# Fused cross-attention and quantized FFN on one core: down products on full chunks, transposed spreading, gate weights scaled ahead of their turn, fewer warming products, a new order in every queue

## What is computed

```python
def _L0_xattn_ref(teacher_logits, teacher_features, Wq, bq, Wk, bk):
    query = einsum('bnc,dc->bnd', teacher_features, Wq) + bq
    key = einsum('bnc,dc->bnd', teacher_features, Wk) + bk
    attention = softmax(einsum('bnd,bmd->bnm', query, key), axis=-1)
    return einsum('bln,bmn->blm', teacher_logits, attention)

def _reorder_quantize_x(x, idx):
    scale = max(abs(x)) / GLOBAL_DIV
    xr = (x / scale)[:, idx]
    scale_x = max(abs(xr), axis=1, keepdims=True) / FP8_MAX
    return _fp8(xr / scale_x), scale_x, scale

def _qlinear(qx, scale_x, scale, W, idx, out_idx=None):
    Wr = W[:, idx]
    w_scale = max(abs(Wr), axis=1, keepdims=True) / FP8_MAX
    y = qx * scale_x @ (_fp8(Wr / w_scale) * w_scale).T * scale
    return y if out_idx is None else y[:, out_idx]

x = x + xattn(layernorm(x), ctx, Wq, bq, Wk, bk)          # x: 4 x 256 x 256, ctx: 4 x 256 x 128
h = layernorm(x)                                          # 1024 rows of 256
g, u = qlinear(h, w_gate), qlinear(h, w_up)               # 704 wide
x = x + qlinear(quantize(silu(g) * u), w_down)            # back to 256 wide
```

## Time and profile before

| | us |
|---|---|
| median of 3 runs | 79.1 (79.03 to 79.25) |
| the profiled execution's own time | 79.58 |
| its span, from the first to the last instruction | 77.8 |
| PE busy (share) | 69.9 (90%) |
| PEld, weight loads | 57.6 (74%) |
| DVE busy | 61.1 (79%) |
| ACT busy | 56.9 (73%) |
| POOL busy | 49.0 (63%) |

### The profile page before, as it was taken

How to read it: one execution, slowest core, us unless ns; L and a number is a source line. 1 busy time by engine, 2 the same in 40 slices (tenths; PEclk the granted TensorE clock), 3 DMA queues, 4 the chain that set the end, 5 groups by cost and what they waited for, 6 DMA issues and landing times.

```text
span 77.8 us, 1587 instructions
## 1 busy us (share of the span) xinstructions
PE 69.9 (90%) x520; PEld 57.6 (74%) x520; DVE 61.1 (79%) x159; ACT 56.9 (73%) x118; POOL 49.0 (63%) x78
## 2 busy tenths in 40 slices
PE   4999999799959999999999999996989979998940
PEld 4999548589938988999887997984765746676710
DVE  1059899899995999988599999808999999992060
ACT  6106899997899889896899997996288371695400
POOL 5103135369649055987989887899998975853330
PEclk9999999999999999999999999999999999999999
DMA  0999899910000000000000011210240101042204
GB/s 13 272 414 418 258 366 412 409 53 8 0 4 4 0 0 0 0 0 8 0 0 0 34 38 34 67 24 1 85 118 0 67 0 56 11 135 71 70 6 135
DMA packets 4088, 6.98 MB, mean 90 GB/s; under 512 B 656, under 2 KB 2448, under 8 KB 4080
## 3 DMA queue, kind: packets, MB, share of 16 engines
q1 hardware_dynamic: 3888, 6.53, 23.5%
q0 software_dynamic: 192, 0.36, 1.4%
HBM read 5.48 MB, written 1.41 MB: 89 GB/s over the span
## 4 chain that ended last, share of the span: by engine, by line
PE 47%; POOL 22%; ACT 12%; issue 9%; DVE 7%; POOLq 0%; DVEq 0%; ACTq 0%
PE gate_ps L1258 9%; POOL act_g L402 9%; POOL wd_scatter L335 8%; PE tT_ps L1086 7%; PE gate_ps L1162 3%; PE up_ps L1137 3%; PE bank_s L1241 3%; PE tT_ps L1209 3%; PE tT_ps L1073 3%; ACT act_g L591 2%; DVE grid_t L769 2%; PE bank_s L1185 2%; DVE y_sb L892 2%; POOL qxT_bf L395 2%; ACT kT L495 2%
## 5 line engine op out<-in xcount | busy, mean ns | idle before, releaser
L402 POOL TENSOR_TENSOR act_g<-act_g,up_scale 128x704 f32<-128x704 f32 x8 | 13.6, 1695 | 1.1 <-ACT act_g L591 1.0
L1162 PE MATMUL gate_ps<-w_hi,qxT 128*128 128x352 f32 x32 | 11.0, 345 | 0.3 <-ACT act_g L591 0.3
L1209 PE MATMUL tT_ps<-ident,sum_t 128*128 128x128 f32 x48 | 10.4, 283 | 0.3 <-ACT tT L613 0.2
L383 POOL TENSOR_TENSOR sum_w<-sum_w,grid_w 128x256 f32<-128x256 f32 x6 | 4.1, 683 | 10.2 <-DVE sum_w L772 10.2
L1162 PE MATMUL gate_ps<-w_lo,qxT 128*128 128x352 f32 x32 | 10.2, 322 | 0.0
L414 POOL TENSOR_TENSOR x_sb<-y_sb,x 128x256 f32<-128x256 f32 x7 | 6.6, 945 | 5.6 <-DVE y_sb L892 5.6
L857 DVE TENSOR_TENSOR t_sb<-up_ps,act_g 128x704 f32<-128x704 f32 x8 | 7.1, 885 | 3.6 <-POOL act_g L402 2.2
L1212 PE MATMUL tT_ps<-negidentb,grid_t 128*128 128x128 bf16 x48 | 9.6, 219 | 0.0
L613 ACT ACTIVATE tT<-tT_ps 128x768 bf16<-128x768 f32 x7 | 5.7, 808 | 4.9 <-PE tT_ps L1212 4.7
L1086 PE MATMUL tT_ps<-attT,xT 128*128 128x256 f32 x32 | 7.6, 381 | 0.9 <-issue 0.9
L548 ACT ACTIVATE grid_w<-wup_sb,s_w 128x256 bf16<-128x256 f32 x12 | 5.2, 497 | 4.3 <-DVE s_w L808 4.3
(11 more groups left out here) (117 smaller groups left out, 203.6 us busy)
## 6 DMA issues: line engine op xcount, KB each, us to landing
wup_sb<-w_gate_up_dram SPq DMA_DIRECT2D x3, 512.0 KB, 4.8
x_sb<-x_dram SPq DMA_DIRECT2D x4, 256.0 KB, 8.0
xT<-x_t_dram SPq DMA_DIRECT2D x2, 512.0 KB, 9.6
out_dram<-x_sb SPq DMA_DIRECT2D x8, 128.0 KB, 1.7
wdn_sb<-w_down_dram SPq DMA_DIRECT2D x1, 704.0 KB, 6.6
head_sb<-head_dram SPq DMA_DIRECT2D x1, 416.0 KB, 5.4
wdnT<-wd_scatter SPq DMA_DIRECT2D x6, 64.0 KB, 1.9
ctx_sb<-ctx_t_dram SPq DMA_DIRECT2D x1, 256.0 KB, 6.8
```

What stands on the lines that cost most here:

```text
L402: nc.gpsimd.tensor_tensor(act_g[:, i % NT], act_g[:, i % NT], up_scale[:, :], ALU.mult)\
L1162: last = nc.tensor.matmul(ps[:, h, 0:IH], qxT[:, b, c, j * P:(j + 1) * P].bitcast(F32R), w[:, c, a, h * IH:(h + 1) * IH].bitcast(F32R), st ...
L1209: nc.tensor.matmul(to, sum_t[:, i % NT, of], ident[:, :], start=True, stop=False, is_transpose=True)
```

## The change

The down products take all 128 partitions of every chunk. For the last chunk the 64 partitions that belong to chunk 4 are multiplied by zeros, which POOL writes once, and `load_down_back(5)` fills the other 64 partitions alone. The products that spread peaks carry the transpose flag. POOL multiplies the rounded gate weights by their peaks (`scale_up`, a TENSOR_SCALAR of 128x256 float32, six of them), so that `turn_up` is four transpositions and two products with the negative identity; the diagonal matrices (128x128, six of them) are gone. WARM_UP is 15 in place of 24. All the lists of calls are in a new order, that of the loads too.

```diff
--- before.py
+++ after.py
@@ -16,7 +16,7 @@
 LN_EPS = 1e-5
 GRID_SHIFT = 20
 LEAST = 1.5 * 2.0 ** -6
-WARM_UP = 24
+WARM_UP = 15
 SCALED_BY_ACT = (0, 3, 6, 7)
 SUMMED = (1, 2, 4, 5)
 
@@ -109,7 +109,6 @@
         grid_w = sb("grid_w", [P, KC, 2, N], BF16)
         sum_w = sb("sum_w", [P, KC, 2, N])
         q_w = sum_w
-        diag_w = sb("diag_w", [P, KC, 1, P])
         w_hi = sb("w_hi", [P, NC, 1, I])
         w_up = sb("w_up", [P, NC, I], BF16)
         qxT_bf = sb("qxT_bf", [P, B, NC, L], BF16)
@@ -233,7 +232,6 @@
         rowscale_done = sem("rowscale_done")
         yscale_done = sem("yscale_done")
         q_w_done = sem("q_w_done")
-        diag_w_done = sem("diag_w_done")
         out_ready = [sem(f"out_ready{i}") for i in range(T)]
 
         block = ctx.enter_context(nc.Block())
@@ -261,7 +259,7 @@
 
                 if k == 0:
                     sp.wait_ge(scattered, 16 * KC)
-                sp.dma_start(wdnT[:, k], wd_dram[chunk(k), :]).then_inc(wdnT_in, 16)
+                sp.dma_start(wdnT[P - fresh[k]:, k], wd_dram[P * k:P * k + fresh[k], :]).then_inc(wdnT_in, 16)
 
             def store(i):
                 sp.wait_ge(out_ready[i], 1)
@@ -274,17 +272,17 @@
                 sp.dma_start(idx_sb[:, :], down_idx).then_inc(idx_in, 16)
 
             load_up(0)
+            load_x(0)
+            load_head()
+            load_x(1)
+            load_ctx()
+            load_down()
+            load_up(2)
             load_up(1)
-            load_head()
-            load_down()
-            load_ctx()
-            load_x(1)
+            load_x(3)
+            load_idx()
             load_x(2)
-            load_x(0)
-            load_up(2)
-            load_idx()
             load_xT(0)
-            load_x(3)
             load_xT(1)
             load_down_back(0)
             load_down_back(1)
@@ -323,6 +321,7 @@
                                              base=0, pattern=[[-1, P]], channel_multiplier=1), "ident")
                 after("ident")
                 nc.gpsimd.tensor_copy(identb[:, :], ident[:, :])
+                nc.gpsimd.memset(wdnT[0:P - fresh[KC - 1], KC - 1], 0.0)
                 nc.gpsimd.tensor_scalar(negidentb[:, :], ident[:, :], -1.0, 1.0, ALU.mult, ALU.mult)\
                     .then_inc(consts_ready, 1)
 
@@ -380,14 +379,13 @@
 
             def subtract_up(k):
                 pool.wait_ge(sum_w_done, k + 1)
-                nc.gpsimd.tensor_tensor(q_w[:, k, 0], sum_w[:, k, 0], grid_w[:, k, 0], ALU.subtract).then_inc(q_w_done, 1)
-
-            def diag_up(k):
-                if k == 0:
-                    after("ident")
+                step(nc.gpsimd.tensor_tensor(q_w[:, k, 0], sum_w[:, k, 0], grid_w[:, k, 0], ALU.subtract), ("q_w", k))
+
+            def scale_up(k):
+                after(("q_w", k))
                 pool.wait_ge(peak_w_done, k // 2 + 1)
-                nc.gpsimd.tensor_scalar(diag_w[:, k, 0], ident[:, :], peak_w[:, k, 0:1], 1.0, ALU.mult, ALU.mult)\
-                    .then_inc(diag_w_done, 1)
+                nc.gpsimd.tensor_scalar(q_w[:, k, 0], q_w[:, k, 0], peak_w[:, k, 0:1], 1.0, ALU.mult, ALU.mult)\
+                    .then_inc(q_w_done, 1)
 
             def copy_qxT(b):
 
@@ -415,69 +413,69 @@
                     .then_inc(out_ready[i], 1)
 
             constants()
-            diag_up(0)
-            diag_up(1)
+            add_eps1(0)
+            subtract_up(1)
             subtract_up(0)
-            diag_up(2)
-            subtract_up(1)
-            diag_up(3)
-            subtract_up(2)
+            scale_up(0)
+            scale_up(1)
             normalise(0)
             normalise(1)
-            add_eps1(0)
             rstd1_of(0)
-            diag_up(4)
+            subtract_up(2)
             normalise(2)
+            add_eps1(1)
+            scale_up(2)
+            normalise(3)
+            add_eps2(0)
             subtract_up(3)
-            add_eps2(0)
-            normalise(3)
+            scale_up(3)
+            subtract_up(4)
+            scale_up(4)
             rstd2_of(0)
-            subtract_up(4)
-            diag_up(5)
+            rstd1_of(1)
             subtract_up(5)
-            add_eps1(1)
-            rowscale_of(0)
             add_eps2(1)
-            rstd1_of(1)
-            copy_qxT(0)
-            rstd2_of(1)
-            rowscale_of(1)
-            scale_act(0)
-            add_eps2(2)
-            copy_qxT(1)
-            scale_act(1)
-            rstd2_of(2)
-            scale_act(2)
+            scale_up(5)
             scatter(0)
             scatter(1)
+            add_eps2(2)
+            scatter(2)
+            rowscale_of(0)
+            rstd2_of(1)
+            scatter(3)
+            copy_qxT(0)
+            scale_act(0)
+            scatter(4)
+            rowscale_of(1)
+            scale_act(1)
+            copy_qxT(1)
+            scatter(5)
+            scale_act(2)
+            rstd2_of(2)
+            yscale_of(0)
+            yscale_of(1)
+            copy_qxT(2)
             rowscale_of(2)
-            scatter(2)
-            copy_qxT(2)
-            scatter(3)
-            scatter(4)
-            scatter(5)
             scale_act(3)
+            yscale_of(2)
+            scale_act(4)
             add_eps2(3)
-            scale_act(4)
+            yscale_of(3)
             rstd2_of(3)
             rowscale_of(3)
-            yscale_of(0)
             scale_act(5)
             copy_qxT(3)
+            yscale_of(4)
             scale_act(6)
             add_residual(0)
-            yscale_of(1)
-            yscale_of(2)
-            yscale_of(3)
+            add_residual(1)
+            yscale_of(5)
             scale_act(7)
-            yscale_of(4)
-            add_residual(1)
+            yscale_of(6)
             add_residual(2)
-            yscale_of(5)
-            yscale_of(6)
             add_residual(3)
+            add_residual(4)
             yscale_of(7)
-            add_residual(4)
             add_residual(5)
             add_residual(6)
...
@@ -1124,7 +1122,8 @@
             def turn_up(k):
 
                 pe.wait_ge(q_w_done, k + 1)
-                pe.wait_ge(diag_w_done, k + 1)
+                if k == 0:
+                    pe.wait_ge(consts_ready, 1)
                 if k >= 2:
                     pe.wait_ge(w_lo_done, k - 1)
                 elif k == 0:
@@ -1134,8 +1133,7 @@
                 for c in range(NC):
                     for a in range(2):
                         if a == 0:
-                            nc.tensor.matmul(wuT_ps[k % 2][:, c, a], q_w[:, k, a, c * P:(c + 1) * P],
-                                             diag_w[:, k, a], start=True, stop=True)
+                            nc.tensor.transpose(wuT_ps[k % 2][:, c, a], q_w[:, k, a, c * P:(c + 1) * P], ident[:, :])
                         else:
                             nc.tensor.matmul(wuT_ps[k % 2][:, c, a], sum_w[:, k, a, c * P:(c + 1) * P], ident[:, :],
                                              start=True, stop=False, is_transpose=True)
@@ -1150,7 +1148,7 @@
                 pe.wait_ge(peak_d_done, 1)
                 for a in range(2):
                     last = nc.tensor.matmul(spread_ps[:, a], peak_d[:, a:a + 1].to_broadcast([P, P]), ident[:, :],
-                                            start=True, stop=True)
+                                            start=True, stop=True, is_transpose=True)
                 last.then_inc(spread_ready, 1)
 
             def product(i, ps, a):
@@ -1183,7 +1181,8 @@
                     pe.wait_ge(exp_done, B)
                 for k in (range(0, HALF_CHUNKS) if h == 0 else range(HALF_CHUNKS, KC)):
                     last = nc.tensor.matmul(bank_s[:, 0, (k % HALF_CHUNKS) * P:(k % HALF_CHUNKS + 1) * P],
-                                            peak_w[:, k, 1:2].to_broadcast([P, P]), ident[:, :], start=True, stop=True)
+                                            peak_w[:, k, 1:2].to_broadcast([P, P]), ident[:, :], start=True, stop=True,
+                                            is_transpose=True)
                 last.then_inc(up_spread, 1)
 
             def up_product(i):
@@ -1238,7 +1237,7 @@
                     pe.wait_ge(y_scaled, i)
                 for k in range(KC):
 
-                    last = nc.tensor.matmul(y_ps[i], tT[P - fresh[k]:, i % 2, k], wdnT[P - fresh[k]:, k],
+                    last = nc.tensor.matmul(y_ps[i], tT[:, i % 2, k], wdnT[:, k],
                                             start=(k == 0), stop=(k == KC - 1))
                 last.then_inc(y_ready, 1)
 
@@ -1247,7 +1246,7 @@
                 if h == 0:
                     pe.wait_ge(qxT_evac, B)
                 for k in (range(0, HALF_CHUNKS) if h == 0 else range(HALF_CHUNKS, KC)):
-                    last = nc.tensor.matmul(y_ps[LAST], tT[P - fresh[k]:, LAST % 2, k], wdnT[P - fresh[k]:, k],
+                    last = nc.tensor.matmul(y_ps[LAST], tT[:, LAST % 2, k], wdnT[:, k],
```

(37 more changed lines are left out.)

191 lines of the change are left out of this document (94 added, 97 removed).

## The result

The changed kernel takes 81.44 us, median of 4 runs (81.06 to 82.2); the kernel before, on the same chip, 79.17 (79.03 to 79.27). The ratio is 1.03, 95% interval 1.0223 to 1.0376: 3% slower. A repeat with three other kernels beside it gave 1.0249 (1.0171 to 1.0326).

What follows compares the result with a forecast made beforehand. The prediction took a shared chain, with everything waiting for POOL in the middle. -0.55 us to the end of `sum_of_t(5)` and -0.4 in the tail sum to -0.95, median forecast 78.2 us; range 76.6 to 80.0.

Steps and rivals of the forecast that it cites:

- the tail: Behind `sum_of_t(5)`: only `down(6)` and the last down product follow the last turn, so 0.4 us less.
- `scale_act(6)` ends at 33.0 + 26.5 + 1.3 = 60.8: POOL's middle: start of `scatter(0)`, plus the sum of POOL's calls, plus hits by DVE sums; `hidden(6)` then at 60.9.
- PE's list has `down(0)` right behind `turn_x(3)`, so PE waits there: PE in the middle: waits for down weights landing at 54.0, reaching `turn_t(5)` at 65.0, 1.1 us below DVE's bound.
- I take 33.0: Start of POOL's first scatter, taken near the late end of 31.8 to 33.6 us.
- signs of being wrong: `scatter(0)` behind 34; DVE idle between 12 and 15; 421 ns PE record behind 6 us; `turn_t(5)` released by PE's queue.
- POOL late by every sum: The second rival: five DVE sum hits of 0.65 and the `rstd` calls delay POOL; +0.7 to +1.1, 80.0 us; chance 0.26.
- The start: Warming products end at 6.1 us, head lands at 6.4, projections start at 6.5, first exponential at about 12.7.
- The gain of 1.65 us: At the start: projections begin at 6.5 us in place of 8.14.
- The scatters ahead of `scale_act(0)` thus buy nothing by themselves: POOL's middle: `hidden(0)` goes from 37.8 to about 41.5 and later tiles catch up; only the down weights come forward.
- The 0.21 us gap: Wait ahead of the 64-row weight load in each down product; full partitions remove it, 8 x 0.21 = 1.7 us less.
- PE's 4 us: Less PE work from transpositions, spreading and full chunks, 4.0 us together; only what lies in the tail counts.
- The stretch from `hidden(6)` to the end of `sum_of_t(5)`: DVE near the end: 5.2 us against 5.8, keeping 0.5 of the grid's stall; ends at 66.1 against 66.65.

Runs made afterwards that it cites:

- c_best: The changed kernel with `grids_x(3)` ahead of `hidden(2)`, `yscale_of(3)` behind `scale_act(5)` and `ups(4)` ahead of `turn_x(3)`; ratio 0.9993 to the kernel before.
- a_grid3: The changed kernel with one DVE call moved, `grids_x(3)` behind `hidden(3)`; ratio 1.0078 to the kernel before.
- c_ups4: The changed kernel with `grids_x(3)` behind `peak_of_t(3)`, `yscale_of(3)` behind `scale_act(5)` and `ups(4)` ahead of `turn_x(3)` and `down(0)`; ratio 1.0027 to the kernel before.
- the two runs: c_best with diagonal matrices back in place of `scale_up`, ratio 0.9969 to the kernel before, and c_rstd, 1.0043.
- a_warm24: The changed kernel with 24 warming products in place of 15; ratio 1.0159 to the kernel before.
- a_oldload: The changed kernel with the loads in their old order and the calls that depend on them moved back; ratio 1.0389 to the kernel before.
- c_late: c_best with the six scatters moved back in POOL's list, two behind each of `scale_act(0)`, `scale_act(1)`, `scale_act(2)`; ratio 1.0283 to the kernel before.
- a_rows64: The changed kernel with the last chunk's down products on 64 partitions again; ratio 1.0255 to the kernel before.
- c_rstd: c_best with one POOL call moved, `rstd2_of(0)` behind `scatter(2)`; ratio 1.0043 to the kernel before.
- b_parts: The kernel before, in its own order, with full down chunks, spreading as transposition and `scale_up` in place of the diagonals; ratio 1.0066 to the kernel before.

## Why the prediction was wrong

**Sum of the error.** Up to the last `scale_y` the forecast was -0.95 us and the profile has +1.40: 2.35 us. `hidden(6)` accounts for 2.1 (63.02 against 60.9), the stretch behind it for -0.2, the tail for 0.4. The 2.1 are three terms: 1.12 for `scatter(0)` (34.12 against 33.0), 0.62 for POOL from there to the end of `scale_act(6)` (28.42 us against 26.5 + 1.3), and 0.38 for DVE's calls between that end and `hidden(6)`, for which the forecast had 0.1. The rest of the medians' difference stays open.

**The step that failed: "`scale_act(6)` ends at 33.0 + 26.5 + 1.3 = 60.8".** It ended at 62.54. The sum took POOL as a queue that never waits, and counted DVE's sums as the only calls that meet it. Not in it was the grid, of which the earlier trace rows had the same case at 1.04 us: `grids_x(3)` stands in DVE's new list between `peak_of_t(2)` and `hidden(3)`, and POOL's has two `scale_act` running there. It took 2.4 us more than in the kernel before, and POOL waited 1.68 us through `yscale_of(3)`. That the stretch came out only 0.62 over is because the rest of it was 1.06 less than summed (the eleven small calls of 0.2 are 2.2, not 2.4, and c_best, without the wait, took 26.95 in all); one error hid part of the other. a_grid3 gives 0.95 back by that one call. Next to it, the step "PE's list has `down(0)` right behind `turn_x(3)`, so PE waits there" named the right place and the wrong wait: the weights were in time, `turn_x(3)` itself was late, and with it `ups(4)`. c_ups4 and c_best give 0.56 more. Together 1.5 us of the 2.35.

**The other step: "I take 33.0" for `scatter(0)`.** It came at 34.12, and by the 28.90 to 28.92 us that follow it in every kernel with these lists, the 1.12 us went through to `hidden(6)` in full. `sums_up(5)` was done at 31.3, 0.8 behind the value that I took and behind its late bound (31.1). And the `rstd` pair, 2.06 us by its rows above where I had 1.7, stands in front: `subtract_up(5)` starts at 32.42, behind it. `subtract_up(4)` took 1.38 through `sum_down(1)`, a hit of 0.7 that was expected. What the sum didn't look at is ACT's piece, which by the 0.86 us of the two runs allows no scatter ahead of 33.94 in this profile. The prediction's own line for the second rival, "from `scatter(0)` at 33.95 on", was crossed. Of its signs of being wrong two came: `scatter(0)` behind 34, and records of 421 ns behind 6 us. No run takes the late scatter away by itself; with it in place (34.02) c_best still has `hidden(6)` at 61.44, 0.5 from the forecast.

**Rival "POOL late by every sum".** It gave `hidden(6)` at 62.2 and 80.0 us, the side on which the result lies, with its late `scatter(0)` and by a mechanism next to the true one: DVE and POOL holding one another, but met by a DVE grid and not by sums alone. It was priced too low, since a hit of a sum costs 0.65 us, while this grid was held for 2.4.

**The start was wrong, and what of it matters isn't the part that I forecast.** I took the array to be on its upper level from 4.8 us and the head to land at 6.4. The warming products ended at 7.5 and the head landed at 7.6: c_best's warming ended by 6.5, and it still waited for the head. PE in order of time, c_best:

```profile
7.61 1.12 PE L1038 MATMUL tT_ps<-head_sb 128*128 128x512 f32 x2 [1.08 <-DMA head_sb<-head_dram]
```

The 4.8 us was misread: it is the first record of the window in the earlier trace rows, and the records had become short at 4.4 already; the count of 30 behind it was right. The sum that had the loads at 417 GB/s failed with the 245 GB/s above. The gain of 1.65 us was 0.5, and DVE waited 1.73 for x; the first exponential came at 14.38, forecast 12.7. The projections don't matter: a_warm24 moves them by 0.87 us and nothing behind. The first exponential does, by the 19.73 to 19.77 us that follow it up to `scatter(0)` in eight kernels. How much of the 1.7 us an early x would give back isn't shown: a_oldload has the early exponential, but DVE's calls stand in another order behind it.

**"The scatters ahead of `scale_act(0)` thus buy nothing by themselves".** Wrong: in c_late they were worth 2.3 us, the start set aside.

**Right.** The 0.21 us gap and its end, against the rule that I had weighed there (the Trainium skill, TensorE: Matmul & The Clock Gate, Part 2, Step-by-step: what each phase is for: row count doesn't matter): the measured rows decide. From the end of `sum_of_t(5)` to the last `scale_y` the old order takes 8.05 us and 7.72 with full chunks, the new one 8.64 in a_rows64 and 8.05 in the changed kernel. That PE's 4 us lie beside other work: all of it together moved the end of the old order by 0.4. The stretch from `hidden(6)` to the end of `sum_of_t(5)`: 5.03 us, forecast 5.2. The tail behind that, forecast 0.4 shorter, took 8.05 us as before (66.65 to 74.70, and 68.05 to 76.10): the full chunks' part was there, but the new order lost as much. The grid at 71.31 took 0.96 us in place of 0.39, under `add_residual`, which would be that size; no run moves it. That DVE and POOL hold one another (the Trainium skill, GPSIMD Engine Reference, 1. Specifications: a shared SBUF interface) fits these rows, with a size that I had not given it. That the interface is what held the grid is argued from calls that overlap in time; what the moves show is that its place cost the time.

## What to carry to other kernels

When an order is changed, lay the queues of DVE and POOL beside each other, call by call: a short DVE call in bfloat16 under POOL calls that follow one another can cost several of them and not its own length, and one move of it was worth 0.8 us here. Then ask for each list what its first late call holds up behind it. An engine that "waits for nothing" in a sum of its calls is an assumption: look for every input of the call at which the sum begins, and at which it ends. And compare two profiles from an event that the edit can't have moved: c_rstd and c_best end alike only because one of them began half a microsecond earlier.

## What the runs showed of the hardware

- The 128x512 bfloat16 grid on DVE takes 0.28 us alone and 2.70 through two `scale_act` that follow one another; the one at 40 us took 2.59 in the changed kernel, through a `copy_qxT` and a `scale_act`, and `scale_act` itself was no longer for it (1.67 and 1.68). Not every grid beside POOL is held so long: the one at 31.21, beside two `rstd`, took 0.28, and the one at 50.58 in c_best 0.29, though a `copy_qxT` began 0.03 us behind it. What decides isn't shown.
- A two-input call of DVE (`sum_down`, 0.94 to 0.95 us) lengthened the POOL call beside it by 0.6 to 0.7 us: `subtract_up(4)` from 0.67 to 1.38 in the changed kernel, `scale_act(0)` from 1.75 to 2.37 in b_parts.
- The warming products went from 421 to 275 ns a record, from the lower to the upper level, at 4.4 us in the kernel before, at 4.2 in c_ups4 and at 7.0 in the changed kernel, where nearly all of the thirty records ran at the lower (6.45 us for 30, 0.215 each), with the same products ahead. The granted clock reads 1.00 from 4 to 6 us in all three. The start of what follows in the kernels of the old order varies with it by 1.1 us (42.64 to 43.77 for the first scatter).
- With x(0) as second load, the rate from 4 to 6 us was 207 to 256 GB/s in eleven profiles; in the five with the old order of loads, a_oldload among them, 413 to 417.
- From the end of the last call to the end of the span passed 2.1 to 2.3 us in the other profiles, but 3.4 in the changed kernel's and 3.2 in a_same, the same kernel; both were the longest of their executions. The cause stays open.
